# Repeating a softmax's exponentials over the head dims: three bf16 parts and one stacked product, or 32-row fp32 products

## What is computed

```python
q = apply_rope((xn @ Wq + bq).reshape(B, T, H, Dh))          # B 8, T 512, H 16, Dh 8
k, v = split(((xn @ Wdown + bdown) @ Wup + bup).reshape(B, T, H, 2 * Dh))
k = apply_rope(k)
att = softmax(einsum('bthd,btgd->bthg', q, k) / sqrt(Dh))    # 16 x 16 for each token
out = einsum('bthg,btgd->bthd', att, v).reshape(B, T, D)     # D 128
x = x + out @ Wout + bout + ffn(xn)
```

## Time and profile before

| | |
|---|---|
| Three runs | 1258.43 us median, 1251.82 to 1283.87 |
| Profiled execution, its own time | 1268.29 us |
| Its span, first to last instruction | 1266.5 us |
| Mean granted clock of TensorE | 0.813 of full speed |
| Busy: PE / DVE / ACT / POOL | 856.6 / 934.0 / 509.3 / 722.6 us |
| Score products of batches 1 to 8 begin at | 37.0 us to 354.7 us |
| Last value product | 435.1 us |
| DMAs into `stack` | 96, of 64 KB each |

### The profile page before, as it was taken

How to read it: one execution, slowest core, us unless ns; L and a number is a source line. 1 busy time by engine, 2 the same in 40 slices (tenths; PEclk the granted TensorE clock), 3 DMA queues, 4 the chain that set the end, 5 groups by cost and what they waited for, 6 DMA issues and landing times. The chain is left out here.

```text
span 1266.5 us, 13006 instructions
## 1 busy us (share of the span) xinstructions
PE 856.6 (68%) x3620; PEld 407.2 (32%) x3620; DVE 934.0 (74%) x1280; ACT 509.3 (40%) x842; POOL 722.6 (57%) x555
## 2 busy tenths in 40 slices
PE   3667888878855717347887878757778777834543
PEld 1123333333322312114544435424444444411210
DVE  3567887798785540176898798859989898969773
ACT  1012312322211103246576585664684574742330
POOL 1022112112106517455778677749998898679996
PEclk9668978998958757767998988978999888955755
DMA  4986666664702123366675766765776777645641
GB/s 126 217 176 154 152 173 174 152 182 109 160 32 83 59 93 121 84 160 198 162 216 178 180 215 167 198 188 125 182 206 162 189 207 173 204 119 112 135 121 29
DMA packets 102835, 192.32 MB, mean 152 GB/s; under 512 B 13131, under 2 KB 68108, under 8 KB 90348
## 3 DMA queue, kind: packets, MB, share of 16 engines
q1 hardware_dynamic: 91500, 183.07, 54.2%
q0 software_dynamic: 11264, 8.43, 3.8%
HBM read 146.80 MB, written 32.06 MB: 141 GB/s over the span
## 5 line engine op out<-in xcount | busy, mean ns | idle before, releaser
L1471 POOL TENSOR_TENSOR hc<-hs,c_rep 128x512 f32<-128x512 f32 x256 | 377.4, 1591 | 114.1 <-DVE hs L1733 113.7
L1726 DVE TENSOR_TENSOR p_du<-p_du,b_rep 128x512 f32<-128x512 f32 x256 | 175.2, 684 | 62.4 <-PE p_du L1839 62.0
L1839 PE MATMUL p_du<-block_in,spread 96*128 96x512 bf16 x256 | 111.4, 441 | 126.8 <-DVE hs L1733 119.5
L1733 DVE TENSOR_TENSOR_SCAN hs<-slots,p_du 128x512 f32<-128x512 f32 x128 | 156.2, 1220 | 40.6 <-POOL hc L1471 27.0
L1733 DVE TENSOR_TENSOR_SCAN hs<-decays,p_du 128x512 f32<-128x512 f32 x128 | 156.2, 1220 | 14.0 <-POOL hc L1471 3.0
L1507 POOL DMA_INDIRECT y_xr<-moe_sums,position x64 | 108.5, 1696 | 39.2 <-issue 25.1
L447 POOL TENSOR_TENSOR sc<-ex,ex_part 128x1024 f32<-128x1024 f32 x8 | 17.0, 2127 | 187.3 <-ACT ex_part L546 187.3
L682 DVE TENSOR_TENSOR value_prod<-p_eb,v 128x512 f32<-128x512 f32 x128 | 83.6, 684 | 37.4 <-PE p_eb L963 37.1
L1607 ACT ACTIVATE decays<-decays,a_neg 128x512 f32<-128x512 f32 x128 | 87.7, 716 | 49.5 <-DMA decays<-dt_rows 49.2
L1848 PE MATMUL p_y<-hc,gather 128*32 128x512 f32 x512 | 83.7, 732 | 35.0 <-POOL hc L1471 35.0
L1839 PEld LDWEIGHTS p_du<-block_in,spread 96*128 96x128 bf16 x256 | 25.4, 100 | 246.2 <-DVE hs L1733 200.8
(11 more groups left out here) (184 smaller groups left out, 1666.2 us busy)
## 6 DMA issues: line engine op xcount, KB each, us to landing
qb<-rq_rows SPq DMA_DIRECT2D x32, 1024.0 KB, 14.1
decays<-dt_rows SPq DMA_DIRECT2D x32, 1024.0 KB
slots<-dt_rows SPq DMA_DIRECT2D x32, 1024.0 KB
wm<-in_wmoe SPq DMA_DIRECT2D x48, 384.0 KB, 13.8
moe_rows<-zeros SPq DMA_DIRECT2D x8, 774.0 KB, 6.3
xg<-moe_rows SPq DMA_DIRECT2D x48, 129.0 KB, 13.7
stack<-ex_part SPq DMA_DIRECT2D x96, 64.0 KB
block_in<-y_part SPq DMA_DIRECT2D x192, 32.0 KB, 5.8
```

The lines of the kernel that those rows point to most:

```text
L1471: nc.gpsimd.tensor_tensor(hc[:, k % NA], hs[:, k % 4], c_rep[:, p], ALU.mult).then_inc(hc_done.sem, 1)
L1726: nc.vector.tensor_tensor(p_du[:, k % 2], p_du[:, k % 2], b_rep[:, p], ALU.mult).then_inc(dbu_done.sem, 1)
L1733: nc.vector.tensor_tensor_scan(hs[:, k % 4], decays[(8 * (b - 1) + k // 4) % NQ][:, bass.ts(j, T)], p_du[:, k % 2], 0.0, ALU.mult, ALU.add ...
L1839: nc.tensor.matmul(p_du[:, k % 2], spread[:, i], block_in[:, (2 * b + s) % NB, j], start=True, stop=True).then_inc(du_full.sem, 1)
```

## The change

The exponentials are repeated by fp32 products of 32 rows that read `ex` where it lies. `over_d` becomes fp32 with one copy for each row group, loaded directly; the three parts, the rest, `stack`, their semaphores and the cast of `over_d` are gone. `ex` gets two buffers. The exponentials of batch b now wait for the spreads and the denominators of batch b - 2, and the copy of the scores waits for the shift of batch b - 1. The order of all remaining instructions is kept.

```diff
-        over_d = sb("over_d", [96, 2, 128], BF16)
+        over_d = sb("over_d", [128, 2, 128])
...
-        ex = sb("ex", [128, 2, T])
-        ex_rest = sc
-        ex_part = sb("ex_part", [128, 3, 2, T], BF16)
-        stack = sb("stack", [96, 2, 4, T], BF16)
+        ex = sb("ex", [128, 2, 2, T])
...
-            def stack_parts(b):
-                sp.wait_ge(eb_full.sem, eb_full.at(b - 1))
-                hold(sp)
-                for i, made in enumerate((part1, part2, part3)):
-                    sp.wait_ge(made.sem, made.at(b))
-                    hold(sp)
-                    for c in range(4):
-                        sp.dma_start(stack[32 * i:32 * i + 32, :, c], ex_part[32 * c:32 * c + 32, i]).then_inc(stacked.sem, 16)
...
-            def first_rest(b):
-                pool.wait_ge(part1.sem, part1.at(b))
-                nc.gpsimd.tensor_tensor(ex_rest[:], ex[:], ex_part[:, 0], ALU.subtract).then_inc(rest1.sem, 1)
-
-            def third_part(b):
-                pool.wait_ge(part2.sem, part2.at(b))
-                pool.wait_ge(rest1.sem, rest1.at(b))
-                pool.wait_ge(stacked.sem, stacked.at(b - 1))
-                nc.gpsimd.tensor_tensor(ex_part[:, 2], ex_rest[:], ex_part[:, 1], ALU.subtract).then_inc(part3.sem, 1)
...
                 act.wait_ge(scored.sem, scored.at(b, 2 * j + 2))
-                act.wait_ge(part3.sem, part3.at(b - 1))
+                act.wait_ge(shifted.sem, shifted.at(b - 1))
...
             def exponentials(b):
                 act.wait_ge(shifted.sem, shifted.at(b))
-                act.wait_ge(den_full.sem, den_full.at(b - 1))
-                act.wait_ge(rest1.sem, rest1.at(b - 1))
-                nc.scalar.activation(ex[:], p_s[:], ACT.Exp).then_inc(exp_done.sem, 1)
-
-            def first_part(b):
-                act.wait_ge(exp_done.sem, exp_done.at(b))
-                act.wait_ge(stacked.sem, stacked.at(b - 1))
-                nc.scalar.activation(ex_part[:, 0], ex[:], ACT.Copy).then_inc(part1.sem, 1)
-
-            def second_part(b):
-                act.wait_ge(rest1.sem, rest1.at(b))
-                nc.scalar.activation(ex_part[:, 1], ex_rest[:], ACT.Copy).then_inc(part2.sem, 1)
+                act.wait_ge(den_full.sem, den_full.at(b - 2))
+                act.wait_ge(eb_full.sem, eb_full.at(b - 2))
+                nc.scalar.activation(ex[:, b % 2], p_s[:], ACT.Exp).then_inc(exp_done.sem, 1)
...
                 if n == 0:
-                    pe.wait_ge(stacked.sem, stacked.at(b))
-                    if b == 1:
-                        pe.wait_ge(setup, SETUP)
+                    pe.wait_ge(exp_done.sem, exp_done.at(b))
                 pe.wait_ge(weighed.sem, weighed.at(b, n - 1) if n >= 2 else weighed.at(b - 1, H - 1 + n))
-                nc.tensor.matmul(p_eb[:, n % 2], over_d[:, hh], stack[:, j, pair], start=True, stop=True).then_inc(eb_full.sem, 1)
+                nc.tensor.matmul(p_eb[:, n % 2], over_d[32 * pair:32 * pair + 32, hh], ex[32 * pair:32 * pair + 32, b % 2, j], start=True, stop=True).then_inc(eb_full.sem, 1)
```

More of the change, by code:

```diff
@@ L93, in constants @@
         sum_e[part, part // H * DH + d] = 1
-    over_d = np.zeros((3, 32, 2, 128), np.float32)
+    over_d = np.zeros((4, 32, 2, 128), np.float32)
     for i in range(2):
@@ L108, in constants @@
         "c_sum_e": sum_e,
-        "c_over_d": over_d.reshape(96, 2, 128),
+        "c_over_d": over_d.reshape(128, 2, 128),
         "c_not_below": not_below,
@@ L257, in layer0 @@
         wd_i = qb[:, 0, 2, 0:FT0 * D].bitcast(I32)
-        over_d_f = qb[0:96, 0, 3, 0:256]
         not_below_f = qb[:, 0, 3, 256:384]
@@ L272, in layer0 @@
                        (sum_d[:], "c_sum_d"), (sum_g[:], "c_sum_g"), (sum_e[:], "c_sum_e"),
-                       (wg_i, "wg"), (wu_i, "wu"), (wd_i, "wd"), (over_d_f, "c_over_d"),
+                       (wg_i, "wg"), (wu_i, "wu"), (wd_i, "wd"), (over_d[:], "c_over_d"),
                        (not_below_f, "c_not_below"), (route_c[:], "c_route"), (wgate[:], "wgate"), (norm_w, "norm_w")]
-        SETUP = 5
+        SETUP = 4
         n_small = len(small_loads) + 1
@@ L353, in _ @@
         def _(sp):
-            start(sp, [*x_in, rq_out, *qb_in, stacked, xr_out, xt2_out, ht2_out])
+            start(sp, [*x_in, rq_out, *qb_in, xr_out, xt2_out, ht2_out])
             sp.dma_start(x[:, 0], x_d[0]).then_inc(x_in[0].sem, 16)
@@ L411, in _ @@
                     repeat_q(b + 1)
-                if b <= B:
-                    stack_parts(b)
                 if b > 1 and b + 3 <= B:
@@ L427, in _ @@
                 sp.wait_ge(into.sem, into.at(B // NX))
-            sp.wait_ge(stacked.sem, stacked.at(B))
             sp.sem_inc(ready1, 1)
@@ L432, in _ @@
         def _(pool):
-            start(pool, [ln_rstd, rest1, part3, pre_root, xr_done, second_set, biased])
+            start(pool, [ln_rstd, pre_root, xr_done, second_set, biased])
             nc.gpsimd.memset(half[:], -0.5).then_inc(made, 1)
@@ L513, in _ @@
         def _(act):
-            start(act, [xt_copied, lat_copied, v_copied, sc_copied, exp_done, part1, part2, gated, xt2_copied, ht2_copied, eg_done])
+            start(act, [xt_copied, lat_copied, v_copied, sc_copied, exp_done, gated, xt2_copied, ht2_copied, eg_done])
             act.wait_ge(loaded0, 16 * n_small)
@@ L593, in _ @@
                     exponentials(b)
-                    first_part(b)
                 if old:
                     gate(b - 1, 0)
-                if new:
-                    second_part(b)
                 if old:
@@ L952, in sum_exp @@
                 for j in range(2):
-                    ins = nc.tensor.matmul(p_a1[64 * j:64 * j + 64], sum_e[:], ex[:, j], start=True, stop=True)
+                    ins = nc.tensor.matmul(p_a1[64 * j:64 * j + 64], sum_e[:], ex[:, b % 2, j], start=True, stop=True)
                 ins.then_inc(den_full.sem, 1)
```

10 lines of the change are left out of this document (removed).

## The result

| | before | after |
|---|---|---|
| Median of four runs each, measured together | 1271.14 us | 1345.01 us |
| Lowest to highest | 1251.82 to 1283.87 | 1341.92 to 1352.24 |
| Ratio after to before, 95% interval | | 1.0724 [1.0637, 1.0812] |
| Profiled span | 1266.5 us | 1339.9 us |
| First layer ends (`tile_expert` of group 1 ends the placing) | 464.0 us | 538.8 us |

A ratio leaves disturbed runs out, which here leaves two runs of the kernel before (1251.82 and 1258.43 us), so it need not be the quotient of two medians. By the ratio the change makes the kernel 7.2% slower, by the medians 5.8%; the time lies outside the range, and the profiled executions differ by 73 us where 24 were forecast. All of it lies in the first layer: 538.8 - 464.0 = +74.8 us, and the second layer is as long as before.

What follows compares the result with a forecast made beforehand. PE's order was taken to bound the first layer's value phase; with overlapping spreads, 27.3 + 4.6 + 2 - 2.9 - 7.1 = +23.9 us gave a forecast of 1282 us, range 1250 to 1312 us.

Steps and rivals of the forecast that it cites:

- PE's order sets the value phase: First layer's value phase: PE works nearly without a gap, so every microsecond put into it moves the iteration's end.
- The price of a spread: On PE, a 32-row fp32 product costs 0.86 us, about 0.1 more per shape change; an overlapping pair 0.96 us.
- One after the other: Rival for the value phase: row groups do not overlap, 6.7 us an iteration, +50 us, 1308 us; chance 0.22.
- In five of the eight iterations spreads 2 and 3 run at the low clock: Value phase: the extra price of these two spreads doubles at the low clock, 5 x 0.4 = 2 us.
- The clock pays: Rival: longer fp32 streams keep PE's clock high through the turns, up to -8 us; 1268 us with partly covered spreads; chance 0.20.
- In steady iterations nobody waits for POOL: First layer: removed subtractions, copies and DMA issues give nothing beyond ACT's 1.05 us.
- Spreads 0 and 1: They cost nothing, standing where PE waits for DVE's score products; otherwise another 0.5 to 1.3 us each time.
- ACT's 1.05 us: Value phase: without the first bf16 part the silu before the second gate product is ready earlier, -1.05 us.
- `rstd`, -2.9: Iteration 1: batch 3's `rstd` no longer stands behind POOL's third part, removing DVE's 2.93 us wait, -2.9 us.
- The scattered writes, -7.1: Iteration 8: POOL's 16 writes start earlier, cutting DVE's 8.94 us wait for the square root by 7.1 us.
- The second layer unchanged: The change touches the first layer alone; the second layer's 800 us stay as they were.
- if steady iterations exceed 52 us: First layer: the forecast's stated failure sign, meaning no overlap or shape changes above 0.1 us; 49 us was expected.

Runs made afterwards that it cites:

- Number 4: The kernel before with each bf16 spread issued four times into the same half of `p_eb`; 1313.95 us, ratio 1.0359 to before.
- Number 1: The kernel after with every spread an fp32 product over all 128 rows, weights zero outside its 32 rows; 1311.32 us, ratio 1.0304 to before.
- number 2: The kernel after with full 128-row fp32 products for spreads 2 to 7 alone, the others at 32 rows; 1310.76 us, ratio 1.0314 to before.
- number 8: The kernel after with spreads of 64 rows, half of the weights zero; 1340.61 us, ratio 1.0478 to before.
- number 9: The kernel after with two overwritten 128-row fp32 products added per iteration, ahead of spreads 2 and 4; 1348.30 us, ratio 1.0517 to before.
- Number 5: The kernel after with POOL's residual made to wait until DVE's `xnr` is done; 1324.19 us, ratio 1.0498 to before.
- Number 6: The kernel before with POOL's residual moved ahead of the first subtraction; 1268.35 us, ratio 1.0059 to before.
- number 10: The kernel before, bf16 spreads kept, with POOL's roots, scattered writes and ACT's gates against the parts reordered; 1251.31 us, ratio 0.9846 to before.
- number 3: The kernel after with bf16 spreads of 32 rows, exponentials rounded once and the other two parts left out; 1276.52 us, ratio 1.0092 to before.

## Why the prediction was wrong, point by point

- **PE's order sets the value phase**: right. Number 4 lengthens nothing but spreads, and a phase at the high level grows from 19.4 to 25.0 us, counted from spread 2.
- **The price of a spread**: right in kind, too low in size. A single spread between full products holds PE for 1.05 us (160.17 to 161.22), forecast 0.96 with its change of shape, and a pair for 1.06 (157.06 to 158.12), forecast 0.96. Rows do overlap: a pair costs no more than one. The Trainium skill (TensorE: Matmul & The Clock Gate, Part 3) says so of row groups, and the trace agrees for two. Counted as the sum counts, from the start of spread 2 and at the high level, the phase takes 24.1 us against 19.4: 4.7, where the sum had 3.9. The windows' 24.7 against 20.8 agrees with 3.9 only by luck: they hang on the maximum, and leave out the 0.75 by which the sum itself has the maxima come later.
- **One after the other**: wrong in its mechanism, and its price was too high as well. Number 1 is that case, each product on all rows: at the high level a phase takes 25.0 us from spread 2, 5.6 more than before and not 6.7. PE has no gap left there (24.8 of 25.0 us busy), and the 2.8 us in which it stood idle before (busy 16.6 of 19.4, "nearly without a gap" in the prediction) took up part of the price.
- **The failed step: "In five of the eight iterations spreads 2 and 3 run at the low clock ... the extra price doubles there, 5 x 0.4 = 2".** The step took from the kernel before that the clock rises behind the first spreads. There the stretch held 96-row bf16 products; with 32-row products the low level lasted through spreads 2 to 7, the sums and the shifts, in five of six iterations until the first gate product. From spread 2 these phases take 29.0 to 29.8 us against 24.1 at the high level, 4.9 to 5.7 us each; all six cost 173.7 - 6 x 24.1 = 29 us, where the sum had 2 (the kernel before pays 118.1 - 6 x 19.4 = 1.7). Numbers 1, 2, 8 and 9 bring the clock back earlier with products of more rows, number 8 with products of exactly the same length.
- **The rival "The clock pays"** had the right quantity and the wrong sign. It reasoned that longer fp32 streams keep PE busy, and so keep the high level. PE was busier than before (27.8 of 28.8 us) and slower.
- **"In steady iterations nobody waits for POOL ... they give nothing"**: true of waits, and blind to order. The subtraction that went had held back POOL's residual; freed, it runs beside `xnr`. This is the second step that failed. The price was nowhere in the sum: 0.9 us of DVE an iteration, and with it a longer gap ahead of the key projection and a clock that is low more often at the phase's start. Number 5 puts it at 20 us of the first layer.
- **Spreads 0 and 1 free**: held, PE still waits for DVE behind them. The stretches, which the prediction called unchanged, grew all the same, by 14.0 / 5 = 2.8 us each when cut at spread 2. Number 6 has the same growth (14.7) with the residual alone, and number 5 takes 11.6 of the 14.0 back, so nearly all of it goes with the residual's place. 0.9 us of the 2.8 is `xnr` itself; how the rest comes about, beyond a granted clock of 0.75 to 0.83 against 0.79 to 0.93, isn't shown, and number 10, whose residual stays in place, also has longer stretches than before (139.9).
- **ACT's 1.05 us**: held. The second gate product no longer waits for ACT. Moved without the fp32 products (number 10) the same step shortens the phase by 1.0 us.
- **`rstd`, -2.9**: half right. POOL does it at 63.34 and `xn` waits no more, but DVE then waits 3.17 us for the denominators, which PE makes at the low clock (64.29, 1.98 us, L905). The next score product starts at 70.63 instead of 72.57 us, 1.9 earlier, of which 0.4 was there at `ve`.
- **The scattered writes, -7.1**: right, the wait is 1.78 us instead of 8.94, though iteration 9 as a whole is 3.6 us longer.
- **The second layer unchanged**: right, 801 against 802 us. **Would be wrong "if steady iterations exceed 52 us"**: they take 56.5 to 59.4, and iteration 8 61.1. The cause is neither of the two that the text named beside it. The 45 to 45.5 us before were read from windows that aren't iterations; from `attn` to `attn` iterations 3 to 7 take 45.3 to 48.8.

Together: of the 74.8 us, the sum had 23.9. What it lacked is about 25 us for the clock in the six phases, 12 for the stretches (14.0, less 1.7 in the last one), 5 for the spreads at the high level (6 x 0.8), and 8 in iteration 9 and behind it (+5.6 where the sum had 4.6 - 7.1 = -2.5).

What stays open: what the stop in iteration 8 of number 8 is; and what in a stretch brings the clock back. In phases entered at the low level it was high again 9 to 14 us after spread 2 with 32-row fp32 products (after; number 5, iteration 3), about 7 us after with the bf16 ones (number 3, iteration 4), and about 4 us after with 64 or 128 rows (numbers 8 and 2, iteration 3) or 96 (before, iteration 4). But in iteration 8 of numbers 8 and 9 it stayed low for 10 and 16 us with 64-row and 128-row products in the stretch, so the number of rows is not the whole account.

## What to carry to other kernels

Before making products smaller in rows, read the level of the clock at which TensorE enters the stretch: products on few rows ran at the high level while it lasted, but it came back late among them, and six of them padded with zero rows to the full height ended the first layer 27 us earlier. Price each removed instruction also by what it holds back on its engine, and look what the freed one will run beside. And take apart a change that mixes gains with a price: the gains of the order alone ended the first layer 9.7 us earlier than before (0.8% of the kernel, 1.5% by the ratio).

## What the hardware showed that I had not expected

- In iteration 3 of after, PE works without a gap from 138.7 us, and its level is low until 156 us, 13 us after the first 32-row pair of the phase began; at 64 rows and the same lengths it is high 3.7 us after that pair began (number 8: 140.88 to 144.62).
- Two phases entered at the low level, both with PE full by the profile: number 4, iteration 4, busy for 25.3 of 25.5 us, has a granted clock of 0.97; after, iteration 3, busy for 27.8 of 28.8, has 0.77.
- Two full-height fp32 products added to a phase at the low level cost nothing: iterations 3 to 7 take 57.8 us on average with them and 58.3 without (number 9).
- DVE's `xnr` is not slowed evenly beside POOL's residual: of its 28 instructions most take 336 ns and the longest 1208, about the residual's own 1.2 us; without it none is above 341 (number 5). The row of line 696 in after (min/median/max ns):

```profile
L696 DVE TENSOR_SCALAR xnr<-x,mv,rr x28: 333/336/1208, 128.0 to 477.2; 128x128 f32<-128x128 f32 x28
```

  The Trainium skill (SBUF — State Buffer, SBUF: two separate sides) describes a port pair shared by DVE and GpSimd: an instruction of either that uses it (some DVE instructions don't) holds it to its end, and the other engine's stands still meanwhile. The trace agrees in form: one instruction of four is about 0.87 us longer, the others are as ever.
